# Attention scores as 32x64 products in four PSUM banks, with the transposes, weighing and output regrouped and the loops reordered

## What is computed

```python
def _attn(x, wq, wk, wv, wo, bq, bk, bv, bo):
    Bb, T, C = x.shape
    hd = C // H
    q = (x @ wq + bq).reshape(Bb, T, H, hd).transpose(0, 2, 1, 3)
    k = (x @ wk + bk).reshape(Bb, T, H, hd).transpose(0, 2, 1, 3)
    v = (x @ wv + bv).reshape(Bb, T, H, hd).transpose(0, 2, 1, 3)
    att = jnp.einsum('bhqd,bhkd->bhqk', q, k) * hd ** (-0.5)
    causal = jnp.tril(jnp.ones((T, T), bool))
    att = jnp.where(causal, att, -jnp.inf)
    att = jax.nn.softmax(att, axis=-1)
    y = jnp.einsum('bhqk,bhkd->bhqd', att, v).transpose(0, 2, 1, 3).reshape(Bb, T, C)
    return y @ wo + bo
```

## Time and profile before

| | |
|---|---|
| median of 3 runs | 1123.22 us (1119.56 to 1129.8) |
| span of the profiled execution | 1125.2 us |
| PE busy | 923.1 us (82%) |
| DVE busy | 774.2 us (69%) |
| ACT busy | 718.9 us (64%) |
| POOL busy | 563.1 us (50%) |
| cross attention, about | 28 to 176 us |
| first self-attention, about | 176 to 345 us |
| second self-attention, about | 590 to 765 us |

### The profile page before, as it was taken

The page is one execution under the profiler, slowest core; times in us unless marked ns, Lnnn a source line. Parts: engine busy times, 40 slices in busy tenths (PEclk is TensorE's granted clock), DMA queues, the critical chain, the costliest instruction groups (busy, mean ns, idle before and its releaser), DMA issues.

```text
span 1125.2 us, 30885 instructions
## 1 busy us (share of the span) xinstructions
PE 923.1 (82%) x10150; PEld 713.2 (63%) x10154; DVE 774.2 (69%) x1936; ACT 718.9 (64%) x1796; POOL 563.1 (50%) x786
## 2 busy tenths in 40 slices
PE   3999989899997279999728888897699999869804
PEld 2677767676675249999715666666477777747601
DVE  4699989899987766666456887766722222857795
ACT  2677767777874457777617887885355555358725
POOL 6455545455655035555377887660233333028715
PEclk9999999999998689999958999997699999889955
DMA  5000031000000202222210000250000000611002
GB/s 137 14 15 14 14 114 48 2 2 0 0 1 3 74 24 66 65 65 65 50 45 25 20 26 21 59 180 1 0 1 0 0 0 0 150 39 39 20 0 75
DMA packets 53187, 41.43 MB, mean 37 GB/s; under 512 B 11176, under 2 KB 45716, under 8 KB 53124
## 3 DMA queue, kind: packets, MB, share of 16 engines
q1 hardware_dynamic: 48220, 31.50, 10.0%
q0 software_dynamic: 4320, 8.86, 3.1%
q10 hardware_dynamic: 584, 0.26, 0.1%
HBM read 27.42 MB, written 9.24 MB: 33 GB/s over the span
## 4 chain that ended last, share of the span: by engine, by line
PE 48%; DVE 17%; ACT 11%; issue 7%; POOLq 7%; POOL 3%; another core or an unknown queue 2%; SPq 2%; DMA 1%; DVEq 0%; ACTq 0%
PE ps_o L1173 10%; PE ps_s L1173 10%; PE ps_t L1262 7%; PE ps_xa L1173 6%; PE ps_v L1173 5%; POOLq L808 5%; PE ps_t L1173 4%; ACT work L926 3%; POOL work L809 2%; DVE rowmax L1652 2%; DVE work L1655 2%; POOLq L798 1%; PE ps_v L1282 1%; ACT shared L917 1%
## 5 line engine op out<-in xcount | busy, mean ns | idle before, releaser
L742 POOL TENSOR_TENSOR shared<-kts,kmask 128x512 f32<-128x512 f32 x192 | 240.4, 1273 | 183.0 <-ACT qts L910 78.7
L934 ACT COPY probs_t<-ps_t 128x1024 f32<-128x1024 f32 x96 | 97.2, 1012 | 65.7 <-PE ps_t L1262 65.1
L770 POOL DMA_INDIRECT xg<-x_rows,row_from x71 | 76.5, 1078 | 112.0 <-PE ps_xa L1343 61.4
L1652 DVE TENSOR_REDUCE rowmax<-ps_s 128x16 f32<-128x1024 f32 x96 | 116.6, 1214 | 20.9 <-PE ps_s L1173 20.8
L1655 DVE TENSOR_TENSOR work<-ps_s,rowmax 128x1024 f32<-128x1024 f32 x96 | 117.5, 1224 | 3.3
L1173 PE MATMUL ps_s<-shared,qts 64*64 64x512 f32 (+1 forms) x896 | 115.5, 584 | 0.7 <-POOL qts L824 0.7
L1262 PE MATMUL ps_t<-ident,work 128*128 128x128 f32 x768 | 105.7, 283 | 8.2 <-ACT work L926 6.7
L1173 PE MATMUL ps_o<-shared,probs_t 128*64 128x18 f32 x3072 | 107.7, 213 | 5.7 <-ACT probs_t L934 5.7
L1173 PEld LDWEIGHTS ps_o<-shared,probs_t 128*64 128x64 f32 x3072 | 98.1, 138 | 17.9 <-ACT probs_t L934 7.3
L926 ACT ACTIVATE work<-work 128x1024 f32<-128x1024 f32 x96 | 100.9, 1051 | 1.4 <-DVE work L1655 1.2
L1262 PEld LDWEIGHTS ps_t<-ident,work 128*128 128x128 f32 x768 | 88.6, 145 | 16.9 <-ACT work L926 16.6
(11 more groups left out here) (368 smaller groups left out, 2237.8 us busy)
## 6 DMA issues: line engine op xcount, KB each, us to landing
...
```

What stands on the lines that cost most here:

```text
L742: i = pool.tensor_tensor(km[:, par, g, :, :], kts[:, par, g:g + 1, :].to_broadcast([P, 8, SEQ]), kmask[:, :, :], ALU.mult)
L770: pool.indirect_dma_start(xg[:, t % XBUFS, :], None, x_d, bass.IndirectOffsetOnAxis(row_from[:, t:t + 1], 0)).then_inc(xg_loaded[t % XBUFS ...
L934: nc.scalar.copy(probs_t[:, par, :], ps_t[:, :]).then_inc(S["pts_ready"], 1)
L1652: V.tensor_reduce(rowmax[:, par, :], s3, AXX, ALU.max).then_inc(S["max_ready"], 1)
```

## The change

The head mask has 4 heads instead of 8 (`KM_HEADS`), so a tile's scores are eight products: two sequences by four groups of 32 channels, 256 columns each. Each group of channels has a bank of its own, four banks (`ps_st`, the former `ps_s` and `ps_t` together), each half filled. The causal mask is two rounds of eight products, for which a second table (`causal_o`) and a padded identity are made at the start. The probabilities are transposed in two halves into `ps_v`, one bank: TensorE can start the second half when ScalarE has copied the first. Weighing, the y transpose and the output projection share `ps_o`, so the weighing of a tile waits for VectorE's addition of the tile before. The v projection goes to `ps_x`, apart from q and k, with waits of its own. `inner_step` moves from ScalarE (one operation) to GpSimd (two, and the bias as before). `norm_step` runs one iteration earlier, the small weights' conversion on VectorE one later, the setup pieces one tile earlier. Row maximum and subtraction are two steps on VectorE, with the addition and `xn` between them.

```diff
-KM_HEADS = 8
+KM_HEADS = 4
+ROWGROUPS = HEADS // KM_HEADS
...
-        ps_s = psum("ps_s", 1024)
-        ps_t = psum("ps_t", 1024)
+        ps_st = psum("ps_st", 2048)
+        ps_s, ps_t = ps_st[:, 0:1024], ps_st[:, 1024:2048]
+        ps_h = ps_st[:, :].rearrange("p (r n) -> p r n", r=ROWGROUPS)
+        ps_h4 = ps_h[:, :, 0:KM_HEADS * SEQ].rearrange("p r (h k) -> p r h k", h=KM_HEADS)
...
@@ routing_constants (GpSimd)
+                fresh(pool.memset(causal_o[:, :, :], 0.0))
+                for r in range(ROWGROUPS):
+                    part = causal_o[r * 32:(r + 1) * 32, :, :]
+                    select(part, [[0, KM_HEADS], [-1, SEQ]], 32 * ((r + 1) % 2), 1, ALU.is_ge, NEG)
...
@@ GpSimd
-            def bias_step(t, par):
-
+            def inner_step(t, par):
+
+                at = tile(inner, t)
+                pool.tensor_tensor(at, tile(x_res, t), rstd[:, bass.ds(t, 1)].to_broadcast([P, D]), ALU.mult
+                                   ).then_inc(S["inner_scaled"], 1)
+                pool.wait_ge(S["inner_scaled"], t + 1)
+                pool.sem_inc(S["pool_begun"], 1)
+                pool.tensor_tensor(at, at, nbias[:, bass.ds(t, 1)].to_broadcast([P, D]), ALU.add
+                                   ).then_inc(S["inner_ready"], 1)
                 pool.wait_ge(S["inner_ready"], t + 1)
...
@@ ScalarE
-                    nc.scalar.copy(probs_t[:, par, :], ps_t[:, :]).then_inc(S["pts_ready"], 1)
+                    act.wait_ge(S["pt_ready"], 2 * ATT[base] + 2 * t + 1 + half)
+                    nc.scalar.copy(probs_t[:, par, 512 * half:512 * half + 512], ps_v[:, :]).then_inc(S["pts_ready"], 1)
...
-                return [(L_OUT, evac_yt(base)), (L_WEIGH, evac_pt(base)), (2, evac_qkv(base, l), VBUFS),
-                        (1, evac_t(base, l, None if l is None else 0, l is None)),
-                        (3, inner_step) if l == 0 else None, (L_SCORES, exp_step(base))]
+                return [(L_OUT, evac_yt(base)), (L_WEIGH, evac_pt(base, 0)), (2, evac_qk(base, l)),
+                        (L_WEIGH, evac_pt(base, 1)), (L_SCORES, exp_step(base)),
+                        (1, evac_t(base, l, None if l is None else 0, l is None)), (2, evac_v(base), VBUFS)]
...
@@ TensorE
-                    for s in range(SPT if masked else 0):
-                        for r in range(2):
-                            h_ = slice(64 * r, 64 * r + 64)
-                            mm(ps_s3[64 * s:64 * s + 64, r, :], identb[h_, h_],
-                               causal[h_, :, :].rearrange("p a b -> p (a b)"), True, False)
+                    for half in range(2 if masked else 0):
+                        for s in range(SPT):
+                            for r in range(ROWGROUPS):
+                                rows_, c = slice(32 * r, 32 * r + 32), 32 + 32 * r - 32 * half
+                                mm(ps_h[64 * s:64 * s + 64, r, 0:KM_HEADS * SEQ], ident_pad[rows_, c:c + SEQ],
+                                   (causal[rows_, 0:KM_HEADS, :] if half == r % 2 else causal_o[rows_, :, :])
+                                   .rearrange("p a b -> p (a b)"), half == 0, False)
                     for s in range(SPT):
-                        for r in range(2):
-                            h_ = slice(64 * r, 64 * r + 64)
-                            i = mm(ps_s3[64 * s:64 * s + 64, r, :], qts[h_, par, s * SEQ:(s + 1) * SEQ],
-                                   km[h_, par, s, :, :].rearrange("p h k -> p (h k)"), not masked, True)
+                        for r in range(ROWGROUPS):
+                            rows_ = slice(32 * r, 32 * r + 32)
+                            i = mm(ps_h[64 * s:64 * s + 64, r, 0:KM_HEADS * SEQ], qts[rows_, par, s * SEQ:(s + 1) * SEQ],
+                                   km[rows_, par, s, :, :].rearrange("p h k -> p (h k)"), not masked, True)
...
-                    pe.wait_ge(S["pts_ready"], ATT[base] + t + 1)
+                    seen(pe, S["x_updated"], UPD[base] + t)
                     for j in range(HEADS // 2):
+                        if j == HEADS // 4:
+                            pe.wait_ge(S["pts_ready"], 2 * ATT[base] + 2 * t + 2)
...
                 return [(L_SCORES, scores(base, l is not None)),
-                        (L_OUT, transpose_y(base)), (L_WEIGH, transpose_probs(base)),
+                        (L_OUT, transpose_y(base)), (L_WEIGH, transpose_probs(base, 0)), (L_OUT, out_project(base, l)),
                         (2, project(base, l)), (1, ctx_transpose(base)) if l is None else None,
-                        (1, transposes(base, nbase)), (L_OUT, out_project(base, l)), (L_WEIGH, weigh(base), VBUFS)]
+                        (1, transposes(base, nbase)), (L_WEIGH, transpose_probs(base, 1)), (2, project_v(base, l)),
+                        (L_WEIGH, weigh(base), VBUFS)]
...
@@ VectorE
-                return [(L_OUT, y_step(base)), (1, norm_step(src, nbase, base, norm)),
-                        (L_SCORES, shift_step(base)), (L_OUT + 1, sums_step(dst, "x_updated", UPD[base])),
-                        (L_OUT, add_step(base, dst, scale))]
+                return [(L_OUT + 1, sums_step(dst, "x_updated", UPD[base])), (L_OUT, y_step(base)),
+                        (L_SCORES, max_step(base)), (L_OUT, add_step(base, dst, scale)),
+                        (0, norm_step(src, nbase, base, norm)), (L_SCORES, shift_step(base))]
...
-                    {2: small_weights,
+                    {3: small_weights,
...
-            y_, _, shift_, sums_, add_ = attention(1, inner, inner, SELF1, rstd, 1.0)
-            straight(later([y_, shift_], LEAD) + [(LEAD, group_rstd), (LAND, combine_first), (LAND, combine_second)]
-                     + later([sums_], LEAD) + [(LAND, fetched_stats)] + later([add_], LEAD))
+            sums_, y_, max_, add_, _, shift_ = attention(1, inner, inner, SELF1, rstd, 1.0)
+            straight(later([sums_, y_, max_, add_, shift_], LEAD)
+                     + [(LEAD, group_rstd), (LAND, combine_first), (LAND, combine_second), (LAND, fetched_stats)])
```

126 lines of the change are left out of this document (72 added, 54 removed).

## The result

In the comparison beside the kernel before, the changed kernel took 1121.14 us (median of 18 runs, 1116.48 to 1128.25) against 1129.03 (18 runs, 1119.39 to 1137.21): ratio 0.9938, 95% interval 0.9909 to 0.9966. On another chip it was 0.9937 (0.9902 to 0.9971). The change gains 0.6%, where 1.7% was forecast. 1121 lies in the range given and within 1% of before, not at 1104.

What follows compares the result with a forecast made beforehand. TensorE was taken to bound the cross attention, its new circle meeting ScalarE's at 4.50 us. Cross 3, first self 10, second self 3 and start 3 make 19 us: span 1125.2 to 1106, as a median 1104; range 1082 to 1136.

Steps and rivals of the forecast that it cites:

- Cross attention, 4.64 to 4.55, 3 us: Cross attention: a tile falls from 4.64 to 4.55 us, saving 3 us over 32 tiles.
- TensorE's circle: TensorE's round in a cross tile, waits for y and the y copy included: 0.73 + 0.75 + 3.02 = 4.50 us.
- First self-attention, 4.97 to 4.65, 10 us: First self-attention: a tile falls from 4.97 to 4.65 us, saving 10 us over 30 tiles.
- what ScalarE gives away is in the circle already: ScalarE: the one activation it loses to GpSimd brings no gain beyond the circle already summed.
- Moved to GpSimd for nothing: GpSimd: the inner norm's three operations run under the next tile's work, needed two tiles later, and cost nothing.
- Second self-attention, 5.78 to 5.65, -3 us: Second self-attention: a tile falls from 5.78 to 5.65 us, saving 3 us on some 24 tiles; bounds 5.0 and 6.2.
- 8.0 every fourth tile: Second self-attention: if both circles add on a table tile, 5.4 + 2.6 = 8.0 us every fourth, giving 6.1 a tile.
- the circle of 5.43: Second self-attention: y, TensorE's round, weighing and late y, with 1.16 us of outside wait, take 5.43 us a tile.
- Start, -3 us: Start: most of the second x transpose's 3.20 us delay behind `xn` goes, saving 3 us; bounds 0 and -4.
- No overlap: Scores, rival: the eight products don't overlap, scores stay 1.02 us; about 1130 us in all, chance 0.18.
- ScalarE's circle grows: ScalarE, rival: its circle sets the pace, with 0.1 us more at each of five hand-overs; 1143 us, chance 0.22.
- Freed: Second self-attention, rival: GpSimd and VectorE stop blocking each other; 5.0 us a tile, 19 us saved, 1088 us, chance 0.18.

Runs made afterwards that it cites:

- e4: Changed kernel with only its scores undone (four products of 64 rows and 512 columns, with their masks and mask product): 1125.15 us, ratio 0.995 to the kernel before.
- e6: Changed kernel with e1_warm's dummy products and the first self-attention's inner norm back on ScalarE, behind the v copies: 1134.86 us, ratio 1.0031 to the kernel before.
- f1: The changed kernel itself, run again on the chip shared with f2 and f4: 1105.17 us, ratio 0.9937 to the kernel before.
- e12: The kernel before with e1_warm's five dummy products added at the start: 1115.89 us, ratio 1.004 to the kernel before without them.
- f4: Changed kernel with dummy products, VectorE's order max, norm, add, shift, and the second self-attention's square root replaced by a copy: 1070.14 us, ratio 0.9597 to kernel before.
- f2: e1_warm again (changed kernel plus the dummy products), on the chip of f1: 1103.11 us, ratio 0.9886 to the kernel before.
- e1_warm: Changed kernel with five dummy 128x512 products in TensorE's idle stretches at the start: 1113.41 us, ratio 0.983 to the kernel before.
- e8: e1_warm with TensorE's output projection moved behind q/k projection and transposes, ScalarE's first-half copy ahead of the y copy: 1146.97 us, ratio 1.0144 to the kernel before.

## Why the prediction was off

- **Cross attention, 4.64 to 4.55, 3 us.** Time right (steady tiles 4.62 to 4.52, 3.2 us), reason half right. The scores were put at 0.55 and the y transpose at 0.73 behind them, since it waits for y; it was 0.76. TensorE's circle as summed would be 4.50, but e4 shows that its pieces were too dear: with scores of 1.02 and no wait at all TensorE needs 4.58, not 4.79. The circle that closes at 4.52 holds add, norm and shift of VectorE between two stretches of the ones I followed. I drew a circle for each engine, and missed the one through three. That its time agrees with the forecast is luck.
- **First self-attention, 4.97 to 4.65, 10 us.** Right in time (4.68, 9.2 us), by luck again: masks cost the lower bound (0.24 for sixteen), TensorE's round of 4.68 was not the limit, the y copy's circle was. And "what ScalarE gives away is in the circle already" left out that the norm adds 0.52 a tile where it stands on that circle (e6).
- **Moved to GpSimd for nothing.** Nothing speaks against it: the tile is the circle's 4.68, without GpSimd, and `xn` fell to 0.34.
- **Second self-attention, 5.78 to 5.65, -3 us.** This step failed: +1.6 in the first pair of traces, +9 between f1 and e12. Averaged over the same 21 tiles it was 5.89 against 5.75. I priced the table loads in the new loop and never asked what they cost in the old one, which on e12's chip takes 5.2 a tile with them. The new one takes 4.78 without them (f4), near ScalarE's circle without loads (4.76). With them four tiles of f1 take 21.85 us, 5.46 each, and 22.82, 5.70 each, where the clock falls, which was put at nothing. The case "8.0 every fourth tile" looked near (8.14, 7.39, 7.37, 8.04 and 7.36 us were measured), but its sum is wrong: 5.4 holds the loads already, so adding 2.6 counts them twice; 4.76 + 2.56 would be 7.3. The outside waits on which I built the circle of 5.43 belonged to the chip.
- **Start, -3 us.** This step failed too, by 8 in the first pair of traces and by 7 in the means of two and three. The second x transpose did come earlier: it starts at 18.29 instead of 22.09, and the first maximum at 26.52 instead of 27.48. What I never asked is what thinner scores and a start with less of TensorE's time in use do to its clock. The dummies bring the sixth tile forward by 7 us (f1 to f2) to 10 us (changed kernel to e1_warm). Which part of the change delays the clock is open; with 64-row scores (e4) it came earlier, in one trace.
- **No overlap** (1130) is refuted by the 0.76. **ScalarE's circle grows** (1143) names the place where the first two stages bind, and e6 and e8 show such growth, but the changed kernel doesn't have it. **Freed** (1088, 5.0 a tile) didn't come: even on the faster chip the changed kernel takes 5.46 to 5.70. f4 shows 4.78, without table loads.
